# Layer 0 without setup blocks and with VectorE rotating its first k, layer 1 projecting two units in a row, layer 3's constants made in layer 2

## What is computed

```python
x = x + _L0_conv_ref(_gn(x), ...)   # retention: rotated q and k, scores times a decay mask, head norm, gelu
x = x + _L1_conv_ref(_gn(x), ...)   # mLSTM: up projection, causal conv of 4 taps, gated linear attention
x = x + _L2_conv_ref(_gn(x), ...)   # neighbourhood attention, 7 x 7 window
x = x + _L3_conv_ref(_gn(x), ...)   # 7 x 7 window attention a soft mask, silu outputs
```

## Time and profile before

| | before |
|---|---|
| median of 3 runs | 3341.45 us (3333.46 to 3352.48) |
| profiled execution | 3342.48 us, span 3340.7 us |
| mean granted TensorE clock | 0.956 |
| PE, DVE, ACT, POOL busy | 90%, 64%, 60%, 34% |

### The profile page before, as it was taken

One profiled execution on the slowest core, in us unless ns is written; L12 is line 12 of the kernel. 1 busy time (PEld: TensorE's weight loads), 2 busy tenths in 40 slices (PEclk: granted clock), 3 DMA queues, 4 the chain that ended last, 5 costly groups with the idle time before them and its releaser, 6 DMA issues. The chain is left out here.

```text
span 3340.7 us, 103137 instructions
## 1 busy us (share of the span) xinstructions
PE 3009.3 (90%) x43288; PEld 1667.2 (50%) x43288; DVE 2137.5 (64%) x5157; ACT 1994.4 (60%) x4348; POOL 1124.1 (34%) x1439
## 2 busy tenths in 40 slices
PE   6999999999986999999999978999985788888886
PEld 2333333333323656556566546676664555555553
DVE  5787787878763667767676744554543466666664
ACT  2667667666663555555555534555552677777774
POOL 3343433434311222122122201222221455555553
PEclk9999999999997999999999989999987999999997
DMA  6777877788672232223323214555443233333332
GB/s 201 162 170 152 177 174 165 155 183 180 133 173 85 67 90 79 72 78 83 87 75 89 73 44 154 161 164 167 149 136 125 70 91 118 113 119 120 112 105 77
DMA packets 298892, 411.55 MB, mean 123 GB/s; under 512 B 39328, under 2 KB 255808, under 8 KB 277824
## 3 DMA queue, kind: packets, MB, share of 16 engines
q1 hardware_dynamic: 275936, 272.53, 27.3%
q0 software_dynamic: 18000, 131.08, 19.6%
q10 hardware_dynamic: 4496, 1.35, 0.2%
HBM read 219.47 MB, written 53.81 MB: 82 GB/s over the span
## 5 line engine op out<-in xcount | busy, mean ns | idle before, releaser
L855 ACT ACTIVATE l_sizes<-l_probs 128x2048 f32<-128x2048 f32 x256 | 487.0, 1908 | 301.7 <-DVE l_probs L804 289.6
L1889 ACT ACTIVATE l_logits<-l_logits,l_low 128x100 f32<-128x100 f32 x1024 | 372.6, 366 | 209.1 <-DVE l_low L1869 208.9
L1896 POOL TENSOR_TENSOR l_logits<-l_logits,l_inv 128x400 f32<-128x400 f32 x256 | 239.6, 937 | 759.2 <-DVE l_inv L1875 758.4
L301 PE MATMUL l_psum<-shared_x,shared_space 128*128 128x512 f32 x896 | 414.9, 609 | 11.1 <-DVE l_row_var L1464 9.2
L804 DVE TENSOR_TENSOR l_probs<-l_psum,l_decay 128x1024 f32<-128x1024 f32 x256 | 299.7, 1219 | 83.5 <-PE l_psum L689 72.9
L804 DVE TENSOR_TENSOR l_probs<-l_psum,shared_space 128x1024 f32<-128x1024 f32 x256 | 300.3, 1219 | 82.5 <-PE l_psum L689 82.0
L689 PE MATMUL l_psum<-l_qk 32*128 32x512 f32 x2048 | 339.5, 643 | 7.0 <-POOL l_qk L941 4.2
L956 POOL DMA_DIRECT2D l_sizes<-l_sizes x125 | 108.7, 869 | 535.2 <-ACT l_sizes L855 523.2
L1708 POOL TENSOR_TENSOR shared_space<-shared_space,l_causal 128x1024 f32<-128x1024 f32 x64 | 152.9, 2390 | 372.9 <-DVE l_x_act L1406 227.4
L704 PE MATMUL l_psum<-l_probs,shared_x 128*32 128x512 f32 x2048 | 269.6, 598 | 0.2
L301 PEld LDWEIGHTS l_psum<-shared_x,shared_space 128*128 128x128 f32 x896 | 164.9, 193 | 199.5 <-issue 193.9
(11 more groups left out here) (242 smaller groups left out, 5723.5 us busy)
## 6 DMA issues: line engine op xcount, KB each, us to landing
l_sizes<-l_sizes POOLq DMA_DIRECT2D x125, 1024.0 KB, 7.6
l_V_windows<-v_image SPq DMA_DIRECT2D x512, 100.0 KB
l_V_windows<-v_padded SPq DMA_DIRECT2D x512, 100.0 KB
shared_space<-rows_c SPq DMA_DIRECT2D x64, 512.0 KB, 5.9
shared_x<-y SPq DMA_DIRECT2D x24, 1024.0 KB, 5.7
y<-l_res SPq DMA_DIRECT2D x31, 512.0 KB, 3.1
l_e_everywhere<-rows_e SPq DMA_DIRECT2D x112, 128.0 KB, 5.7
shared_x<-x SPq DMA_DIRECT2D x8, 1024.0 KB, 11.0
```

The lines of the kernel that those rows point to most:

```text
L301: i = nc.tensor.matmul(out, w[:, k, m * P:(m + 1) * P], act[:, k, n0:n1], start=(k == 0), stop=(k == tiles - 1))
L855: nc.scalar.activation(sizes[:, slot(N), :, :], probs[:, N % 2, :, :], ACT.Abs).then_inc(sized, 1)
L1889: nc.scalar.activation(e, e, ACT.Exp, scale=-1.0, bias=self.low[:, N % 4, i:i + 1], accum_out=self.total[:, N % 4, i:i + 1]).then_inc(self ...
L1896: nc.gpsimd.tensor_tensor(p, p, self.inv[:, N % 4, :].unsqueeze(2).to_broadcast([P, STEP, NKEY]), ALU.mult).then_inc(self.p_ready, 1)
```

## The change

Three places are changed.

1. Layer 0's two setup blocks and their barrier are gone. Every load is issued in the main block: SP sends x[0], `wq`, `wv`, the rotation table, the two decay halves, image 1, in that order; ACT sends `group_mean`, `wk`, `wo`, `row_scale`, `ln_g`, `ln_b`, `head_mean`. PE waits for `first_loaded` (group_mean, wk, wq). VectorE, ScalarE and GpSimd wait for `rest_loaded` to reach 112, all seven other constants. VectorE makes the mean-free `wv` in its own stream, behind image 0's statistics and ahead of the rotation, and `wv_ready` lets PE project v. VectorE also does the whole rotation of the first k (`finish_first_key`), GpSimd that of the first q alone.
2. In layer 1 the function `layer1_ups(u)` says which units are projected up at step u: 0 and 1 at u = -2, none at -1, u+2 from 0 on. PE, ScalarE's `up`, VectorE's `convolve` and GpSimd's `border` follow it.
3. Layer 3's constants live in a class `Constants3` made ahead of layer 2. Layer 2's SP sends nine of them at its start, GpSimd zeroes them and both key images in steps 6 to 8 of batch 1, VectorE casts at step 8, and SP zeroes the padded value images (2 x 1.44 MB) at step 9. Layer 3's waits for all this are gone.

```diff
-        load_all(nc, L, [ ... ])
-        with nc.Block() as block:
-            @block.vector
-            def _(dve):
-                nc.vector.memset(ones[:, :], 1.0)
...
-        L.barrier_and_clear()
-        vstep.restart()
...
                 load(0)
+                sp.dma_start(wq[:, :, :], wview(A["L0_WqT"])).then_inc(first_loaded, 16)
+                sp.dma_start(wv[:, :, :], wview(A["L0_WvT"])).then_inc(rest_loaded, 16)
+                sp.dma_start(table[:, :], A["rot_table"]).then_inc(rest_loaded, 16)
...
+                pe.wait_ge(first_loaded, 48)
                 for name in layer0_order()[0:4]:
+                    if name[0] == "v":
+                        pe.wait_ge(wv_ready, 1)
                     fill(name)
...
+                def finish_first_key():
+                    dve.wait_ge(sw_ready, 4)
+                    ring.is_taken(dve, ("k", 0))
+                    for a in range(2):
+                        s = slice(a * BANK, (a + 1) * BANK)
+                        vstep(dve, nc.vector.tensor_tensor(by_row(sw[:, 1, s]), by_row(sw[:, 1, s]), turned(1, a), ALU.mult))
+                    nc.vector.tensor_tensor(qk[:, 0, 1, :], qk[:, 0, 1, :], sw[:, 1, :], ALU.add).then_inc(rot_done, 1)
...
                 norm.collect(nc, dve, ring, 0)
+                nc.vector.memset(ones[:, :], 1.0)
+                dve.wait_ge(rest_loaded, 112)
+                heads = wv[:, :, :].rearrange("p k (h d) -> p k h d", d=HD)
+                vstep(dve, nc.vector.tensor_reduce(wmean[:, :, :], heads, axis=AX.X, op=ALU.add))
+                vstep(dve, nc.vector.tensor_scalar(wmean[:, :, :], wmean[:, :, :], 1.0 / HD, 0.0, ALU.mult, ALU.add))
...
+                act.wait_ge(rest_loaded, 112)
                 values(0)
...
                 apply(0)
+                pool.wait_ge(rest_loaded, 112)
                 rotate(("q", 0))
-                rotate(("k", 0))
...
+def layer1_ups(u):
+    return (0, 1) if u == -2 else (u + 2,) if 0 <= u < UNITS - 2 else ()
...
+                for dst, src in c3.loads(A):
+                    sp.dma_start(dst, src).then_inc(c_loaded, 16)
                 for j in range(4):
                     store_values(0, j)
...
+                        if (b, n) == (1, 9):
+                            sp.wait_ge(keys_cleared, 1)
+                            for s in range(2):
...
+                    if b == 1 and n in (7, 8):
+                        i = nc.gpsimd.memset(c3.keys[8 - n][:, :, :], 0.0)
...
-                dve.wait_ge(rest_loaded, 176)
...
-                act.wait_ge(consts_ready, 1)
```

More of the change, by code:

```diff
@@ L548, in layer0 @@
         next_loaded = L.sem("next_loaded")
+        first_loaded, rest_loaded, wv_ready = L.sem("first_loaded"), L.sem("rest_loaded"), L.sem("wv_ready")
         def wview(w):
             return w.rearrange("(k p) n -> p k n", p=P)
[L553 to L559, removed]
-        with nc.Block() as block:
-            @block.vector
-            def _(dve):
-                nc.vector.memset(ones[:, :], 1.0)
[L564 to L568, removed]
-        L.barrier_and_clear()
-        vstep.restart()
         def by_row(ap):
@@ L1684, in _ @@
                     if t == 3:
-                        if 0 <= p < UNITS:
+                        for p in layer1_ups(u):
                             up(p, 0)
@@ L1763, in _ @@
                     if t == 3:
-                        if p % 2 and 0 <= p < UNITS:
-                            border(p)
+                        for p in layer1_ups(u):
+                            if p % 2:
+                                border(p)
                         if 0 <= n < UNITS:
@@ L1768, in layer1, with __init__, sb, loads @@
         L.barrier_and_clear()
+class Constants3:
+    def __init__(self, shared):
+        def sb(name, shape, dt=F32):
+            return shared.new("l3_" + name, shape, dt)
+        self.b_wp, self.pair, self.w_on, self.w_qk = sb("b_wp", [P, 2]), sb("pair", [P, 2]), sb("w_on", [P, HALVES]), sb("w_qk", [P, 2])
+        self.head_mean, self.all_mean, self.dist = sb("head_mean", [P, P]), sb("all_mean", [P, P]), sb("dist", [P, NKEY])
+        self.outside, self.pick = sb("outside", [P, STEP * NKEY], BF16), sb("pick", [P, 32], BF16)
+        self.eps4 = sb("eps4", [P, 1])
+        self.keys = [sb(f"keys{s}", [P, HALVES, IMAGE * IMAGE]) for s in range(2)]
+        self.raw_outside = shared.space[:, 1664:1664 + STEP * NKEY]
+        self.raw_pick = shared.space[:, 1664 + STEP * NKEY:1664 + STEP * NKEY + 32]
+    def loads(self, A):
+        return [(self.b_wp[:, :], A["L3_b_wp"]), (self.pair[:, :], A["pair"]), (self.w_on[:, :], A["L3_w_on"]),
+                (self.w_qk[:, :], A["L3_w_qk"]), (self.head_mean[:, :], A["head_mean"]), (self.dist[:, :], A["dist"]),
+                (self.raw_outside[0:16, :], A["outside"]), (self.raw_outside[64:80, :], A["outside"]), (self.raw_pick, A["pick"])]
 class Tiles:
@@ L2134, in _ @@
                         residual(b - 1, 1, n - 3)
+                    if (b, n) == (1, 8):
+                        dve.wait_ge(c_loaded, 16 * len(c3.loads(A)))
+                        dve.wait_ge(c_ready, 1)
+                        for r in range(2):
+                            rows = slice(64 * r, 64 * r + 16)
+                            nc.vector.tensor_copy(c3.outside[rows, :], c3.raw_outside[rows, :])
+                        nc.vector.tensor_copy(c3.pick[:, :], c3.raw_pick)
+                        nc.vector.scalar_tensor_tensor(c3.w_qk[:, 0:1], c3.w_qk[:, 0:1], HD ** -0.5 / GAIN, c3.w_qk[:, 1:2], ALU.mult,
+                                                       ALU.mult)
                     if 10 <= n < 14 and b + 1 < B:
```

95 lines of the change are left out of this document (40 added, 55 removed).

## The result

The changed kernel takes 3317.14 us (median, 3301.20 to 3327.70) beside 3332.43 us for the kernel before on the same chip: a ratio of 0.9943, 95% interval 0.9924 to 0.9962. (The ratios here are estimates over all executions of both kernels, not quotients of the two medians, which would be 0.9954.) The prediction was 3319 us. The profiled execution took 3324.22 us (span 3322.4) at a mean granted clock of 0.955; that of before 3342.48, at 0.956. Of the 18.3 us between these two, layer 3 alone gives 20.6, layer 0 takes 1.9, and layers 1 and 2 come out even. The predicted sum, 22.4, had 18.1 in layer 3, 4.3 in layer 1, 0.5 in layer 0 and -0.5 in layer 2. So I read the four starts again.

What follows compares the result with a forecast made beforehand. PE, busy 90% on average and nearly full inside layers 1 and 2, idles at the four layer starts. Terms 18.1 + 4.3 + 0.5 - 0.5 = 22.4 us off 3342.48 give 3320.1, so 3319 as median; range 3304 to 3328.

Steps and rivals of the forecast that it cites:

- Layer 3, predicted +18.1: Layer 3's start: VectorE's zeroing, casts and constant wait vanish, v's projection starts earlier; gain 18.1 us, bounds 15 and 18.5.
- Layer 2, predicted -0.5: Layer 2: nine small DMAs, zeroing, memsets and casts added there cost 0.5 us, bounds 0 and 7.
- Layer 1, predicted +4.3: Layer 1's start: PE gets the second unit's gates earlier, without copies ahead of decay; gain 4.3 us, bounds 0 and 5.
- The rival that it is absorbed: Layer 1: the first units' head start is absorbed, PE's order of later units being the same; 3323.5 us, chance 0.06.
- Layer 0, predicted +0.5: Layer 0's start: first scores 0.8 us later, clock giving back 1.3; gain 0.5 us, bounds -2 and +3.5.
- The main step: Layer 0: VectorE waits for all seven constants, the last, `head_mean`, coming with SP's last row at 32 us.
- the clock's +1.3: Layer 0: v's projection directly ahead of the scores may bring them full clock; up to 4 us saved, 1.3 taken.
- The rival "full gain": Layer 0: small rows pass the large ones, constants there by about 10 us; gain 12.7 us, 3307 us, chance 0.14.
- the 9.1 for the image: Layer 0, in the full-gain rival: image and projection come early, 9.1 us of its 12.7.
- the 3.6 for k's rotation: Layer 0, in the full-gain rival: k's rotation beside q's saves 3.6 us of its 12.7.
- The slowdown through the clock in layer 1: Layer 1: shifted starts make PE fall to half clock more often; 0.5% slower needs a mean of 0.92, chance 0.03.

Runs made afterwards that it cites:

- no_l3: The changed kernel with the third edit undone, layers 2 and 3 as they were before: 3341.40 us, ratio 0.9994 to the kernel before.
- consts_first: The changed kernel, but SyncE issues decay halves and image 1 only after all seven constants landed: 3299.29 us, ratio 0.9905; timed again 3314.99 us, 0.9937.
- own_waits: The changed kernel with every transfer in place, but one semaphore split in three so each engine waits for its own constants: 3314.33 us, ratio 0.9929.
- consts_first_one_unit: The changed kernel with decay table and image 1 issued behind the constants and layer 1's edit undone: 3307.68 us, ratio 0.9911.

## Why the prediction was right, and where it was not

**Layer 3, predicted +18.1, measured 18.3 at the start** (20.13 - 1.87). The layer as a whole lasts 781.4 us on average over the three executions with the old code and 761.1 over the eleven with the new: 20.3, with a standard deviation of about 5 us in a single one. The 20.6 of the profiled pair is therefore no sign of a further gain. This term alone accounts for what can be measured: no_l3, which keeps the edits in layers 0 and 1, can't be told from the kernel before.

**Layer 2, predicted -0.5, measured 0.** Over the same two groups its mean is 540.0 and 539.9 us. The two memsets that went to GpSimd took 2.5 us each, under the 2.9 that a step has free; the nine issues held SP for 8.7 us instead of 4.1, but delayed the gathers by 1.1 us, of which 0.4 reached PE at the start and none the end. The size of that term came out right although SP's part in it was priced at half.

**Layer 1, predicted +4.3, measured 3.9 at the second gates of the profiled pair, 3.3 on average (59.6 us in ten executions with the edit, 62.8 in four without), its survival open.** The steps came as written: silu(0) 1.0 us later (predicted 0.6), `mask` 1.0 later, two masks in a row, `decay` for both chunks without copies between. Whether the layer is shorter is not settled. By the table it is 1008.9 us on average without the edit (four) and 1006.1 with it (ten), which leans to the prediction's side, but the difference of 2.8 is smaller than the standard deviation of 5 us of a single execution; and the two timed comparisons contradict each other. The rival that it is absorbed stays possible.

**Layer 0, predicted +0.5, measured -1.9 in the profiled pair.** The main step held: VectorE waited for all seven constants, and `head_mean` released it at 30.70 where I had 32. The scores were predicted at 41.9 and came at 42.08, but by errors that cancel. The constants were 1.3 us early and the swaps 0.5 us shorter, and k's finish took 4.8 us instead of 2.8: its two multiplications needed 3.45 us, not 1.4, while GpSimd worked beside them. I had priced them by the cosine products (0.67 each), which read one operand from PSUM; the sine products read both from SBUF. Alone they cost the same (0.69 in consts_first); the rest is time in which they wait for GpSimd's addition and row scale to end. The Trainium skill, "GPSIMD Engine Reference", section "Specifications", names that case: an instruction of VectorE with two SBUF inputs contends with GpSimd for their common interface. The trace agrees, with 3.45 us for the pair and 2.24 instead of 1.91 for GpSimd's row scale. The step that failed is the clock's +1.3: v's projection ahead of the scores, mostly at half clock itself after PE's idle 9.69 us (6.37 us at a mean of 0.59, before 3.73 at 1.00), brought no full clock, and 42 to 51 us went at 0.50 where 0.54 had been before. Over several executions the term drowns: layer 1 begins at 1015.2 us on average in the four with this layer 0, and at 1014.4 and 1019.4 in the two of before.

**The rival "full gain", 12.7 us, did not come, and its sum was about right.** Of its two terms the 9.1 for the image came out at 9.75, and the 3.6 for k's rotation at 2.2. What kept it away was one wait. With it gone the scores are 11.7 to 13.7 us earlier, and layer 1 begins at 1001.5 us on average (six executions) instead of 1015.2. The slowdown through the clock in layer 1 did not come: 0.96 as before, in the stretch of the earlier trace rows.

**That 3319 came within 2 us of the measured 3317.14 is partly luck.** It was counted down from the three executions of the kernel before that I had (median 3341.45), and the fourteen beside the result have 3332.43; the same 22.4 us taken from that give 3310. What can be compared is the change: 22.4 of 3341.45 is a ratio of 0.9933, inside the measured 0.9924 to 0.9962.

The sum was 4.1 us better in the forecast than in the profiled pair (22.4 against 18.3): 2.4 in layer 0, 4.7 in layer 1, 0.5 back in layer 2 and 2.5 in layer 3, each of these within what two executions of one kernel differ by.

**The better version** is own_waits or consts_first: ratios of 0.9929, 0.9905 and 0.9937, where the changed kernel has 0.9943 and 0.9951. The intervals overlap, and the changed kernel was not timed beside own_waits, so the whole does not show a gain; but in all four of their profiles, consts_first_one_unit's among them, the scores are 11.7 us or more earlier. That so much of it reaches the end is likely, since layer 1 begins 13.7 us earlier on average, and not shown.

## What to carry to other kernels

One semaphore for "all constants" makes every engine wait for the slowest of them. Before a load is moved in beside large transfers, ask which constant each waiter really needs, give it its own count, and count rows, not bytes: a queue of tiny rows beside one with 30 KB rows moves at the pace of the large ones. Before work is moved from GpSimd to VectorE, look at what GpSimd does at that moment: here a product with both operands in SBUF cost 0.69 us alone and up to 2.28 behind a GpSimd instruction. And when an edit is worth 0.1%, read it at the place where it acts and in several executions, since the total of one says nothing about it.

## What the runs showed that I had not expected

- In the changed kernel a transfer of 0.5 KB (ln_g, 128 rows of 4 bytes) took 22.2 us from issue to landing beside the decay table.
- VectorE's multiplication of a swapped half by the sine took 0.69 us with GpSimd idle, and 2.11 and 2.28 us when it started beside GpSimd's row scale: it ended 0.54 to 0.55 us after GpSimd's instruction in all four cases looked at. The cosine product over the same 512 columns, with one operand in PSUM, took 0.67 to 0.68 either way.
- A unit of layer 1 lasts 56 to 57 us or about 59, by whether a half-clock stretch falls into it; executions of one kernel differ by up to 41 us (3318.22 to 3359.13 over 29 of the kernel before, on one chip).
